# Full-row scores for layer 1, and the order of the first twenty slots, in a two-layer transformer kernel

## What is computed

```
x  = x + attn0(norm(x)) + ffn0(norm(x))      # 16 heads of 128, causal; ffn0 in bf16/fp8, 1024 hidden
x  = x + attn1(norm(x)) + ffn1(norm(x))      # 16 heads of 16; ffn1 with Hadamard transforms, 1024 hidden
# attn1, per head:
q, k, v = (x @ W + b).reshape(b, l, 16, 16)
a = softmax(einsum('blhd,bLhd->bhlL', q, k) / 16)
out = einsum('bhlL,bLhd->blhd', a, v) @ Wo + bo
```

## Time and profile before

| | us |
|---|---|
| median of 3 runs | 902.43 (901.55 to 903.78) |
| the profiled execution, own time | 901.08 |
| its span, first to last instruction | 899.3 |
| TensorE busy in the span | 820.1 |
| VectorE busy | 699.8 |
| ScalarE busy | 691.9 |
| GpSimd busy | 478.0 |

### The profile page before, as it was taken

The page is one execution under the profiler, slowest core; times in us unless marked ns, Lnnn a source line. Parts: engine busy times, 40 slices in busy tenths (PEclk is TensorE's granted clock), DMA queues, the critical chain, the costliest instruction groups (busy, mean ns, idle before and its releaser), DMA issues.

```text
span 899.3 us, 21251 instructions
## 1 busy us (share of the span) xinstructions
PE 820.1 (91%) x7136; PEld 609.2 (68%) x7136; DVE 699.8 (78%) x2011; ACT 691.9 (77%) x1997; POOL 478.0 (53%) x751
## 2 busy tenths in 40 slices
PE   3776887899999999999999999999999999976875
PEld 1334665677777777777777777777777777754653
DVE  6988786687888787878787878788878887886763
ACT  3787695666787888788878888788778877886563
POOL 4701465334465555556564665466546655585473
PEclk9899899999999999999999999999999999999896
DMA  9332676223356666558546774576358555866354
GB/s 294 132 114 97 144 187 151 48 37 87 74 104 81 114 121 106 83 115 127 107 82 107 125 117 75 106 125 115 75 104 137 100 91 87 131 94 126 73 106 82
DMA packets 283341, 98.62 MB, mean 110 GB/s; under 512 B 241249, under 2 KB 278881, under 8 KB 282849
## 3 DMA queue, kind: packets, MB, share of 16 engines
q1 hardware_dynamic: 283232, 97.27, 56.8%
HBM read 30.11 MB, written 8.39 MB: 43 GB/s over the span
## 4 chain that ended last, share of the span: by engine, by line
PE 66%; DVE 13%; ACT 5%; DMA 3%; issue 3%; POOL 2%; SPq 1%; POOLq 0%; ACTq 0%; DVEq 0%
PE ps L784 40%; PE ps L867 8%; PE ps L975 4%; PE ps L958 3%; DVE arena L778 3%; PE ps L828 3%; DMA arena<-arena 2%; DVE arena L1199 2%; PE ps L986 2%; ACT arena L1054 2%; DVE arena L777 2%; PE ps L960 2%; PE ps L880 2%; ACT arena L773 1%; DVE nb L1206 1%
## 5 line engine op out<-in xcount | busy, mean ns | idle before, releaser
L778 DVE SCALAR_TENSOR_TENSOR arena<-ps,bqk,arena 128x256 bf16<-128x256 f32 x416 | 187.2, 479 | 47.9 <-ACT arena L773 47.0
L784 PE MATMUL ps<-arena,wqkv 128*128 128x256 bf16 x1728 | 217.2, 276 | 0.0
L773 ACT ACTIVATE arena<-ps,bqk 128x256 bf16<-128x256 f32 x416 | 177.8, 465 | 28.1 <-PE ps L784 17.5
L784 PEld LDWEIGHTS ps<-arena,wqkv 128*128 128x128 bf16 x1728 | 163.0, 99 | 42.1 <-issue 21.1
L1404 POOL TENSOR_SCALAR arena<-arena,rc 128x128 f32<-128x128 f32 (+1 forms) x256 | 105.4, 424 | 147.9 <-DVE rc L1222 147.9
L1054 ACT ACTIVATE arena<-arena,nb 128x128 f32<-128x128 f32 (+1 forms) x256 | 114.3, 447 | 83.1 <-DVE nb L1199 82.7
L1395 POOL TENSOR_TENSOR arena<-arena 128x512 bf16<-128x512 f32 x115 | 136.2, 1186 | 67.6 <-ACT arena L772 67.5
L1411 POOL TENSOR_SCALAR arena<-arena,rc 128x256 f32<-128x256 f32 x256 | 119.0, 477 | 59.2 <-DVE rc L1226 59.0
L772 ACT ACTIVATE arena<-arena 128x384 bf16<-128x384 f32 (+1 forms) x256 | 136.4, 572 | 12.2 <-DMA arena<-arena 7.0
L1054 ACT ACTIVATE arena<-ps,nb 128x256 f32<-128x256 f32 x256 | 118.5, 473 | 17.6 <-DVE nb L1206 15.4
L867 PE MATMUL ps<-wo,arena 128*128 128x256 bf16 x768 | 105.3, 273 | 14.9 <-DVE arena L778 14.2
(11 more groups left out here) (111 smaller groups left out, 1215.7 us busy)
## 6 DMA issues: line engine op xcount, KB each, us to landing
arena<-scratch_qk SPq DMA_DIRECT2D x84, 64.0 KB, 2.8
arena<-arena SPq DMA_TRANSPOSE x256, 3.1
scratch_qk<-arena SPq DMA_DIRECT2D x28, 128.0 KB, 1.9
arena<-in_x SPq DMA_DIRECT2D x4, 512.0 KB, 9.6
arena<-in_w_gating SPq DMA_DIRECT2D x4, 512.0 KB, 8.3
arena<-in_w_q SPq DMA_DIRECT2D x4, 512.0 KB, 4.9
arena<-in_w_k SPq DMA_DIRECT2D x4, 512.0 KB, 5.8
arena<-in_w_v SPq DMA_DIRECT2D x2, 1024.0 KB, 6.5
```

What stands on the lines that cost most here:

```text
L773: return nc.scalar.activation(out, in_, ACT.Identity, bias=bias)
L778: return nc.vector.scalar_tensor_tensor(out=out, in0=in_, scalar=bias, in1=hi, op0=ALU.add, op1=ALU.subtract)
L784: last = nc.tensor.matmul(out, lhsT, rhs, start=(n == 0), stop=(n == len(steps) - 1))
```

## The change

- Layer-1 scores contract over all 128 rows. `qs` is laid out as (8 pairs of heads, 2, T): the copy for the even head has zeros on the odd head's rows and the other way round. It is no longer double-buffered, so q is stacked in two halves (`stack_q(b, 0)` and `stack_q(b, 1)`, six DMAs each). GpSimd zeroes `ks` in slot 14 and `qs` in slot 18. The masked q of the last batch moves to `sp0`.
- In slots below 20, `proj_qk0` alternates between two banks, and TensorE does `proj_qk0(s)` ahead of `scores0(s-1)`.
- `p0_low` of the first 20 heads moves from VectorE to GpSimd.
- Of the chunks split in slots, the high part of half 1 is written by VectorE (`copy_high`) ahead of `split_low_dve`, not by ScalarE.
- VectorE's `fold(s)` moves from the head of the slot to behind `qk0_low(s)`.
- The broadcast of `sc_u` (1 MB) is cut into four loads in slots 8 to 11 (before: one, in slot 10); `sc_d` moves from slot 10 to 12.

```
+        qs = carve(H1 * T // 2, BF16, "p (h e t) -> p h e t", e=2, h=H1 // 2)
+        ks = carve(2 * H1 // 2 * T // 2, BF16, "p (b h t) -> p b h t", b=2, h=H1 // 2)
...
+        def copy_high(dve, c, j):
+            staged(dve, c)
+            if c[0] == "dn":
+                dve.wait_ge(dn_sums, 2)
+            s, hi, _ = half(c, j)
+            nc.vector.tensor_copy(hi, s).then_inc(chunk_copied, 1)
...
+        TWO = 20
+        def bank_qk0(n):
+            return BK_M if n < TWO and n % 2 else BK_QK
...
-                    r = 64 * (h % 2)
                     for i in range(TT):
                         last = nc.tensor.matmul(ps[:, bank, i * T:(i + 1) * T],
-                                                qs[r:r + 3 * HD1, b % 2, h // 2, i * P:(i + 1) * P],
-                                                ks[r:r + 3 * HD1, b % 2, h // 2, :], start=True, stop=True)
+                                                qs[:, h // 2, h % 2, i * P:(i + 1) * P],
+                                                ks[:, b % 2, h // 2, :], start=True, stop=True)
...
+                if s < TWO:
+                    proj_qk0(s)
                 if 0 <= s - 1 < NG0:
                     scores0(s - 1)
...
-                if s < NG0:
+                if TWO <= s < NG0:
                     proj_qk0(s)
...
-                for c in splits_in[s]:
-                    split_high(act, c, 1)
...
             for s in range(SLOTS):
                 last = s >= NG0
-                fold(s)
...
-                if 0 <= s - 2 < NG0:
+                if EARLY <= s - 2 < NG0:
                     p0_low(s - 2)
...
                 if s < NG0:
                     qk0_low(s)
+                fold(s)
...
                 for c in splits_in[s]:
+                    copy_high(dve, c, 1)
                     split_low_dve(dve, c, 0)
...
+            def p0_low(n):
+                pool.wait_ge(p0_hi, n + 1)
+                nc.gpsimd.tensor_tensor(pb0[:, n % 2, 1, :], sp0[:, n % 3, :], pb0[:, n % 2, 0, :], ALU.subtract
+                                        ).then_inc(p0_early, 1)
...
+                if s == 14:
+                    weights_ready(pool, ("l1", 0))
+                    nc.gpsimd.memset(ks[:, :, :, :], 0.0).then_inc(ks_zero, 1)
+                if s == 18:
+                    weights_ready(pool, ("wo1", 0))
+                    nc.gpsimd.memset(qs[:, :, :, :], 0.0).then_inc(qs_zero, 1)
...
+                if 8 <= s < 12:
+                    n = slice(512 * (s - 8), 512 * (s - 7))
+                    sp.dma_start(scu[:, n], t["sc_u"][n].partition_broadcast(P)).then_inc(scale_loaded[s - 8], 16)
```

More of the change, by code:

```diff
@@ L185, in build @@
         split_tile = {("qk", 0): 14, ("v", 0): 20}
+        act_halves = [(c, j) for c in splits for j in range(2) if c in split_tile or j == 0]
+        dve_halves = [(c, 1) for c in splits if c in split_slot]
         load_slot = {("qk", 2): 1, ("qk", 3): 2, ("wo0", 1): 4, ("ug", 0): 5, ("ug", 1): 7, ("l1", 0): 8, ("dn", 0): 9,
                      ("wo1", 0): 10}
+        scale_loaded = [sem(f"scale_loaded{i}") for i in range(4)]
         stage_loaded = [sem(f"stage_loaded{i}") for i in range(STG)]
@@ L699, in build @@
         pieces_in = by_slot(piece_slot, B * 3)
+        seconds_of_q = {start1(b) + 12: b for b in range(LASTB)}
         turns_in = by_slot(turn_slot, B)
@@ L749, in build @@
         rows_ready = [sem(f"rows_ready{i}") for i in range(2)]
-        spilled, stacked = ([[sem(f"{n}_{w}{i}") for i in range(2)] for w in "qk"] for n in ("spilled", "stacked"))
+        spilled = [[sem(f"spilled_{w}{i}") for i in range(2)] for w in "qk"]
+        stacked_q, stacked_k = ([sem(f"stacked_{w}{i}") for i in range(2)] for w in "qk")
+        qs_zero, ks_zero = sem("qs_zero"), sem("ks_zero")
+        p0_early = sem("p0_early")
         stored, q_masked, masks_ready = sem("stored"), sem("q_masked"), sem("masks_ready")
-        qm = qs[:, LASTB % 2].rearrange("p (e a m) t -> p e a m t", e=2, a=2)
+        qm = sp0[:, :, :].rearrange("p r c -> p (r c)")[:, 0:4 * T].bitcast(BF16).rearrange(
+            "p (e a m t) -> p e a m t", e=2, a=2, m=KD)
         def free_m(pe, kind, n):
             last = before_m.get((kind, n))
-            if last is not None:
+            if last is None:
+                pe.wait_ge(qk0_lo, TWO)
+            else:
                 pe.wait_ge((exp1, x1T_lo, qkv1_lo, o1_lo)[last[0]], last[1] + 1)
@@ L762, in weights_ready, with p0_split @@
             eng.wait_ge(stage_free[number[c] % STG], frees_upto[c])
+        EARLY = 20
+        def p0_split(eng, n):
+            if n < EARLY:
+                eng.wait_ge(p0_early, n + 1)
+            else:
+                eng.wait_ge(p0_lo, n + 1 - EARLY)
         def p1_split(eng, n):
@@ L804, in scores1 @@
                 if h == 0 and b < LASTB:
-                    for w in range(2):
-                        pe.wait_ge(stacked[w][b % 2], 96 * (b // 2 + 1))
+                    pe.wait_ge(stacked_k[b % 2], 96 * (b // 2 + 1))
+                if h % 8 == 0 and b < LASTB:
+                    pe.wait_ge(stacked_q[h // 8], 96 * (b + 1))
                 if h == 0 and b == LASTB:
@@ L841, in proj_qk0 @@
                 for w in range(2):
[L842 removed]
+                    last = group(ps[:, bank_qk0(n), w * T:(w + 1) * T],
                                  [(wqkv0[:, a, w, k, g * HD0:(g + 1) * HD0], cur[:, b % 2, c, k, :])
@@ L1443, in pool_program @@
                         p1_low(n)
+                if 0 <= s - 2 < EARLY:
+                    p0_low(s - 2)
                 if 0 <= s - 1 < NG0:
@@ L1489, in spill @@
                 if b:
-                    sp.wait_ge(stacked[w][(b - 1) % 2], 96 * ((b - 1) // 2 + 1))
+                    if w == 0:
+                        for j in range(2):
+                            sp.wait_ge(stacked_q[j], 96 * b)
+                    else:
+                        sp.wait_ge(stacked_k[(b - 1) % 2], 96 * ((b - 1) // 2 + 1))
                 for a in range(2):
```

65 lines of the change are left out of this document (43 added, 22 removed).

## The result

The changed kernel takes 909.92 us (median of 7 runs, 907.58 to 913.25), against 903.78 (901.55 to 905.87) for the kernel before on the same chip. The ratio is 1.0069, with a 95% interval of 1.0045 to 1.0093: slower by 0.7%. The forecast was 905.8, with a range of 889 to 912; its side was right, its size 4 us short.

A forecast was written before the change was run, and what follows sets the result against it. TensorE's own sequence was taken to bound 200.84 to 788.40 us, with the bound changing by slot before; -16.0 + 13.9 + 1 + 4.5 = +3.4 on 901.08 gave 904.5 profiled, 905.8 as median; eight-in-ten range 889 to 912.

The forecast's parts named there:

- slots 0 to 11: Early slots: copies and a TensorE hole cost time, quartered load and early projection save it; +1 us, bounds -4 to +6.
- windows 12 to 20, the ring: Fold behind `qk0_low` plus early `proj_qk0` close one dependence ring across engines; 63.60 us against 49.70, +13.9.
- the clock in them: In the fold slots, TensorE's idle time lets its clock fall three times; +4.5 us, bounds 0 and +8.
- saturated stretch, without the second stack: Slots 28 to 123: full-row scores save 0.20 us per head, 19.2, less 4.4 lost to `o0_low` waits; -14.8 us.
- the second stack in SyncE's queue: Six more q DMAs in slot 12 of a batch, ahead of `turn0` and `turn1`, cost nothing; 0 us.
- behind slot 123: 12 more shape switches where TensorE is idle a quarter of the time, half their gain taken; -1.2 us.
- the hole ahead of `project_out0`: Early slots: TensorE waits for `o0_low` without `proj_qk0` to fill the time; +1.5 us over windows no copy binds.
- The zero fills: GpSimd's two fills, slots 14 and 18, 3.8 us each: hidden, or up to 1 us each beside fold and `p0_low`.
- 3, faster: Early slots are set by VectorE's and ScalarE's amount of work, so shed work pays; 890 us, chance 0.35 with partial forms.
- 4: Layer-1 scores: 128-row products still pay the 0.20 us, since something other than shape causes it; 922 us, chance 0.02.
- 2, a clock that holds: Clock stays at 2.4 GHz through the folds, no change; 901.3 us, chance 0.24 together with sums of small deviations.
- 1, collisions at the shared port: Early slots: VectorE's eight copies each wait for GpSimd's `norm_0` or `p0_low`; +5.6 us, 911, chance 0.09.

The follow-up runs named there:

- e3: Changed kernel with the second q stack's six DMAs issued behind the slot's two transposing DMAs: 901.78 us, ratio 1.0005 to the kernel before.
- e5: Changed kernel with fold at slot head, one q/k bank and old TensorE order, both high halves on ScalarE, second q stack behind transposes: 890.73 us, ratio 0.9835.
- e6: e5 with `p0_low` back on VectorE and `sc_u` loaded at once, leaving full-row scores, zero fills and the late second stack: 891.27 us, ratio 0.9843.
- e9: e5 with VectorE's copies of the second halves put back: 892.57 us, ratio 0.9853 to the kernel before.
- e11: e10 with GpSimd's two zero fills moved behind its fold of the slot: 885.51 us, ratio 0.9793; the version to keep.
- e2: Changed kernel without the second q/k bank and without `proj_qk0` ahead of `scores0`; VectorE's fold stays late: 896.68 us, ratio 0.9931.
- e4: Changed kernel with both high halves of a split chunk written by ScalarE again: 909.59 us, ratio 1.0051 to the kernel before.
- e12: Changed kernel with GpSimd's two zero fills moved behind its fold of the slot: 910.22 us, ratio 1.0066 to the kernel before.
- e10: e5 with `p0_low` of the first 20 heads back on VectorE: 886.19 us, ratio 0.9805 to the kernel before.

## Why the prediction came out as it did

By stretches of the profiled executions (us), the start and the end of the run apart:

| step | predicted | measured |
|---|---|---|
| slots 0 to 11 | +1 | +1.5 |
| windows 12 to 20, the ring | +13.9 | +12.9 |
| the clock in them | +4.5 | +4.3 |
| saturated stretch, without the second stack | -14.8 | -14.4 to -16.1 (e3, e5, e6, e9 to e11) |
| the second stack in SyncE's queue | 0 | +6.0 |
| behind slot 123 | -1.2 | +0.8 |

- **The folds.** The mechanism and its size were right. Each window with its clock at full is within 0.2 us of its sum: 6.89 for 6.99, 7.76 for 7.87, and 19 and 20 came out at 5.98 for 6.17 and 5.32 for 5.42. Taken at full clock the nine windows sum to 62.6, against 63.6. e2 took the one link out and the ring lost just that link.
- **The clock.** Three falls were forecast, and three came: in windows 12, 16 and 18, each 1.4 to 1.5 us above the same ring at full clock (8.32 to 6.89, 9.19 to 7.76, 7.93 to 6.45), 4.3 in all. The exact count was luck. With the same ring e3 had one, longer fall (window 16, 10.65 us at 0.68, 2.9 us lost), e4 three, and e12 four with 7.3 us lost in all. So the term lies between 2.9 and 7.3 in four executions.
- **The scores.** 0.20 us per head, from the two gaps in the timeline, was exact; that the columns set the cost and zeros are free held too. Of the 96 windows with a head 20 (e6) or 21 (e3) gained nothing, where 22 were forecast to lose their gain to the wait for `o0_low`. The 1.2 behind slot 123 is not shown: that stretch varies by 2.4 us among these kernels.
- **The step that failed**, though the time fell inside the range, is "slots 9 and 10 already hold six such DMAs each and TensorE is not idle there, so I take nothing". It compared DMA counts and not positions. The question was what stands behind the six issues in slot 12, when it is needed, and with how much slack. The issues take 2.9 us or more and `attend1` had less than that to spare. How much less isn't set by the time of the issues alone: with some 2.9 us of them window 60 grew by 0.74 and window 108 by 1.25. The term was 6 us in place of 0, in the saturated stretch, where all of it counts. With it the sum would have been +9.4, or 910.5 for the profiled execution, which took 911.85. The rest is as large as the later start of `max_0(0)`, 1.3.
- **Slots 0 to 12.** The sum was right by luck: its parts weren't. The forecast let the copies bind (+4.9) and the hole ahead of `project_out0` add 1.5 elsewhere. In the trace the hole binds in windows 4 to 6 (1.04, 0.80 and 0.65 us over before, with the copies or without them, e4); the copies cost 2.6 us in six windows when it is gone (e9). The quartered load was worth 4.2 us in one pair of executions (e10, e6), against 3.3 forecast, with a cost before that varies; the longest wait of `attend0` for a transposing DMA up to 200 us is 1.8 in the changed kernel, and was 2.88. The early projection, credited with 2.1 us in two windows at half clock, shows in one: window 1 is 5.5 to 5.8 us in the five kernels that have it, and 5.9 to 7.6 in the nine that don't. Window 3, by the clock, was 8.11 us in the changed kernel and 6.43 in e3 and e12, so the sum itself moves by 1.7 us from one execution to another.
- **The zero fills** were said to be hidden, or up to 1 us each with a fold beside them. That holds for the changed kernel, whose late emptying hides them (e12). In the order of before one of them costs 2.5 us; the bound was too low, for the same reason as with the stack: what stands behind it was not followed to `max_0`.
- **The rivals.** 3, faster, was to be decided by windows 12 to 20 under 59 us; they took 66.9. 4 falls by the gaps that closed. 2, a clock that holds, falls by 0.79, 0.81 and 0.78. 1, collisions at the shared port, falls by copies of 0.68 us, and for the reason that the prediction gave against it: at the end of the slot `norm_0` is mostly over.

Still open: why the clock falls in one, three or four of the same windows from one execution to another, and what makes the single load of `sc_u` cost 4 us at one time and almost none at another.

## What to carry to other kernels

An order that lets one engine start early can close a ring through its other work. Add up the links from one instruction to its next turn, on paper, and a window comes out to 0.2 us or better; it costs nothing to do this before moving a step. When DMAs or a long fill are put into an engine's queue, ask what stands behind them there and how long it can wait, not how many there are: both misses here were of this kind. And among full-row products one that uses part of the rows pays at both edges, so padding with zeros may be the cheaper form.

## What the hardware showed that was not expected

- 64 rows out of 128 cost the same 0.20 us per pair of products as 48 did (waits of 23.6 us over 106 weight loads on the way in, and 23.8 over 113 on the way out, in both); 128 rows cost none.
- The clock fell in windows of which TensorE was busy for some two thirds (5.59 of 8.32 us, 6.46 of 9.19, 5.42 of 7.93), in pieces with waits of 0.92 to 1.14 and of 1.59 us between them. In all three falls it is the "up" piece behind the wait of 1.59 that first takes 1.89 us. This is window 16 of the changed kernel, where "up" took 1.89 us and "down" 1.65, and not the 1.04 of the window before:

```profile
188.67 1.89 PE L820 MATMUL ps<-wug,had_u 128*128 128x512 bf16 x4 [1.59 <-DVE arena L1359]
190.35 1.65 PE L820 MATMUL ps<-wdn,had_d 128*128 128x256 bf16 x8
```

  e2's windows have the same gap of 1.59 us before the same product, but are 1.3 us shorter, and there the clock held in every one. In the changed kernel it held in window 14, which has that gap too, and in 13, 15 and 17, where a v piece fills the hole and the wait before "up" is 0.29.
- Six DMA issues in SyncE's queue took 2.8 us in one batch and 4.2 in another of the same execution.
